# Output stage of a two-layer gated attention kernel: early low parts on VectorE, down bias on GpSimd

## The reference, cut to what matters

```python
def _bit_quant(w):
    scale = jnp.maximum(jnp.mean(jnp.abs(w)), EPS)
    return jnp.clip(jnp.round(w / scale), -1.0, 1.0)      # in the forward pass

# end of _L1_xattn_ref
x = x + jnp.tanh(g_xattn[1]) * (attn @ Wo.T + bo)
# _L1_ffn_ref(_layernorm(x))
h = jnp.einsum('bsd,fd->bsf', ln, _bit_quant(w1)) + b1     # 2048 hidden
h = jax.nn.gelu(h, approximate=False)
x = x + jnp.tanh(g_ffn[1]) * (jnp.einsum('bsf,df->bsd', h, _bit_quant(w2)) + b2)
```

## Time and profile before

| | us |
|---|---|
| three runs | 2008.91, 2006.67, 2000.90 |
| their median | 2006.67 |
| the profiled execution, its own time | 1998.72 |
| its span in the trace | 1996.9 |
| TensorE matmuls busy (share of the span) | 1913.5 (96%) |
| VectorE busy | 998.1 (50%) |
| ScalarE busy | 752.5 (38%) |
| GpSimd busy | 1098.9 (55%) |

### The profile page before, as it was taken

The page is one execution under the profiler, slowest core; times in us unless marked ns, Lnnn a source line. Parts: engine busy times, 40 slices in busy tenths (PEclk is TensorE's granted clock), DMA queues, the critical chain, the costliest instruction groups (busy, mean ns, idle before and its releaser), DMA issues. The chain is left out here.

```text
span 1996.9 us, 29500 instructions
## 1 busy us (share of the span) xinstructions
PE 1913.5 (96%) x10300; PEld 1606.3 (80%) x10300; DVE 998.1 (50%) x1670; ACT 752.5 (38%) x1147; POOL 1098.9 (55%) x986
## 2 busy tenths in 40 slices
PE   8999999999999999989999899998999997999998
PEld 6888888988888888967777799998777775778886
DVE  5446444745466444663333333333888876771111
ACT  4327343644336332632121221222444454434333
POOL 6765688549756777454116855640544435833333
PEclk9999999999999999999999999999999997999999
DMA  5231332223322423334136755532898666240000
GB/s 175 85 116 54 117 116 95 75 86 127 105 80 69 148 85 126 115 134 163 40 117 202 245 170 186 155 109 73 250 258 227 180 170 219 87 127 21 21 21 21
DMA packets 172283, 248.10 MB, mean 124 GB/s; under 512 B 44992, under 2 KB 69568, under 8 KB 172160
## 3 DMA queue, kind: packets, MB, share of 16 engines
q1 hardware_dynamic: 157072, 202.09, 32.1%
q0 software_dynamic: 9472, 34.09, 5.1%
q10 hardware_dynamic: 5616, 10.23, 1.3%
HBM read 179.77 MB, written 66.58 MB: 123 GB/s over the span
## 5 line engine op out<-in xcount | busy, mean ns | idle before, releaser
L262 POOL TENSOR_TENSOR a_w_hl<-a_w_raw,a_w_hl 128x512 fp32r<-128x512 f32 x232 | 303.9, 1342 | 140.9 <-ACT a_w_hl L341 140.9
L477 PE MATMUL a_proj<-a_c_hl,a_w_hl 128*128 128x512 f32 x768 | 180.5, 394 | 9.1 <-DVE a_w_hl L597 8.7
L477 PE MATMUL a_proj<-a_w_hl,a_c_hl 128*128 128x512 f32 x768 | 181.2, 392 | 0.0
L551 PE MATMUL a_proj<-a_w_hl,a_a_hl 128*128 128x512 f32 x768 | 178.7, 391 | 0.8 <-DVE a_a_hl L681 0.8
L477 PEld LDWEIGHTS a_proj<-a_c_hl,a_w_hl 128*128 128x128 f32 x768 | 144.1, 189 | 41.5 <-DVE a_w_hl L597 10.9
L477 PE MATMUL a_proj<-a_a_hl,a_w_hl 128*128 128x512 f32 x768 | 176.4, 390 | 0.0
L371 ACT ACTIVATE a_sq<-a_proj,a_vecs 128x512 f32<-128x512 f32 x128 | 88.1, 688 | 212.9 <-PE a_proj L477 143.5
L2642 POOL TENSOR_TENSOR f_a_hl<-f_act_sb,f_a_hl 128x512 fp32r<-128x512 f32 x64 | 86.1, 1347 | 148.9 <-ACT f_a_hl L2690 148.8
L477 PEld LDWEIGHTS a_proj<-a_a_hl,a_w_hl 128*128 128x128 f32 x768 | 143.6, 188 | 29.7
L341 ACT ACTIVATE a_w_hl<-a_w_raw 128x2048 fp32r<-128x2048 f32 x59 | 112.8, 1911 | 144.8 <-PE a_proj L477 106.7
L551 PEld LDWEIGHTS a_proj<-a_w_hl,a_a_hl 128*128 128x128 f32 x768 | 142.9, 188 | 30.2 <-issue 1.2
(11 more groups left out here) (269 smaller groups left out, 3494.5 us busy)
## 6 DMA issues: line engine op xcount, KB each, us to landing
a_w_raw<-in_a_vi_w SPq DMA_DIRECT2D x16, 1024.0 KB, 4.9
a_w_raw<-in_a_q_w SPq DMA_DIRECT2D x16, 1024.0 KB, 4.9
a_w_raw<-in_a_o_w SPq DMA_DIRECT2D x16, 1024.0 KB, 5.3
a_w_raw<-in_a_ki_w SPq DMA_DIRECT2D x15, 1024.0 KB, 5.7
spare<-in_b_gate_up POOLq DMA_DIRECT2D x32, 352.0 KB, 3.3
l_sorted_rows<-b_zeros SPq DMA_DIRECT2D x39, 256.0 KB, 3.7
spare<-l_sorted_rows SPq DMA_DIRECT2D x39, 256.0 KB, 3.2
l_expert_out<-spare ACTq DMA_DIRECT2D x39, 256.0 KB, 3.5
```

The costliest lines, as they stand in the source:

```text
L262: ins = pool.tensor_tensor(w_hl[:, s, 1, k], w_raw[:, s, k], f32(w_hl[:, s, 0, k]), ALU.subtract)
L477: mm = pe.matmul(proj[:, j, :], left, right, start=(k == 0 and n == 0), stop=(k == KC - 1 and n == 2))
L551: mm = pe.matmul(proj[:, j, :], a_hl[:, ap, k, j * P:(j + 1) * P], w_hl[:, i % 2, wp, k], start=(n == 0 and m == 0), stop=(n == 4 * G - 1 ...
```

## The change

Three things are altered in `l1_output_ffn`.

1. The low parts of chunks 4 to 7 are computed by VectorE (`early_low_part`) behind the statistics of tile 1, with a semaphore of their own (`a_early`), and no longer by GpSimd. The counts that SyncE and TensorE wait for are adapted.
2. The scaled down bias is added to the rows by GpSimd inside the feed-forward loop, tile m - 1 of the block ahead of the low part m, for m = 1 to 4. VectorE's addition behind the multiply-add goes away; its multiply-add now waits for GpSimd's addition (`y_biased`), and the store for the multiply-add (`y_added`).
3. Ahead of the loop GpSimd waits for the last normalised tile (`ln_done` 16) and for the scaled down bias (`const_done` 2).

```diff
--- before.py
+++ after.py
@@ -2518,6 +2518,8 @@
         a_in = [sem(f"a_in{s}") for s in range(RING)]
         a_high = sem("a_high")
         a_split = sem("a_split")
+        a_early = sem("a_early")
+        y_biased = sem("y_biased")
         o_ready = sem("o_ready")
         o_added = sem("o_added")
         ln_stats = sem("ln_stats")
@@ -2535,7 +2537,6 @@
         g_split = sem("g_split")
         y_ready = sem("y_ready")
         y_added = sem("y_added")
-        y_done = sem("y_done")
         x_out = sem("x_out")
 
         x2_t = x2.rearrange("(b n p) d -> b p n d", p=P, n=TPB)
@@ -2564,7 +2565,10 @@
             def load_chunk(n):
 
                 if n >= KC + RING:
-                    sp.wait_ge(a_split, n - RING + 1)
+                    if n - RING < AHEAD:
+                        sp.wait_ge(a_early, n - RING - KC + 1)
+                    else:
+                        sp.wait_ge(a_split, n - RING - (AHEAD - KC) + 1)
                 sp.dma_start(a_raw[:, n % RING, :], a_t[n % KC][n // KC]).then_inc(a_in[n % RING], 16)
 
             def load_piece(m):
@@ -2593,7 +2597,7 @@
                 load_piece(m)
             with sp.Fori(0, NBLK) as t:
                 for j in range(TPB):
-                    sp.wait_ge(y_done, TPB * t + j + 1)
+                    sp.wait_ge(y_added, TPB * t + TPB + j + 1)
                     sp.dma_start(out_t[j][t], y[:, bass.ds(TPB * t + j, 1), :]).then_inc(x_out, 16)
             sp.wait_ge(x_out, 16 * NT)
 
@@ -2623,8 +2627,6 @@
             pool.wait_ge(const_done, 1)
             add_bias(0)
             add_bias(1)
-            for n in range(KC, AHEAD):
-                a_low(n)
             for n in range(NT + 2):
                 if n < NT:
                     pool.wait_ge(ln_eps, 2 * n + 2)
@@ -2636,8 +2638,13 @@
                     add_bias(n + 2)
                 for m in chunk_beside(n):
                     a_low(m)
+            pool.wait_ge(ln_done, NT)
+            pool.wait_ge(const_done, 2)
             with pool.Fori(0, NBLK) as t:
                 for m in range(NG * FC):
+                    if 0 < m <= TPB:
+                        tile = y[:, bass.ds(TPB * t + m - 1, 1), :].rearrange("p a d -> p (a d)")
+                        pool.tensor_tensor(tile, tile, tg_b2[:], ALU.add).then_inc(y_biased, 1)
                     pool.wait_ge(g_high, NG * FC * t + m + 1)
                     pool.tensor_tensor(a_hl[:, 1, m % FC, :], act_sb[:, m % 2, :], f32(a_hl[:, 0, m % FC, :]),
                                        ALU.subtract).then_inc(g_split, 1)
@@ -2696,8 +2703,12 @@
             pe.matmul(m_ps[:], ones[:], sum2[:], start=True, stop=True).then_inc(mean_ready, 1)
 
             def project_out(n):
-                if n:
-                    pe.wait_ge(a_split, KC * (n // TPB + 1))
+                if n >= 2 * TPB:
+                    pe.wait_ge(a_split, KC * (n // TPB + 1) - (AHEAD - KC))
+                elif n >= TPB:
+                    pe.wait_ge(a_early, AHEAD - KC)
+                elif n:
+                    pe.wait_ge(a_split, KC)
                 if n >= 2:
                     pe.wait_ge(o_added, n - 1)
                 own = slice(n * P, (n + 1) * P)
@@ -2812,9 +2823,18 @@
                 dve.tensor_tensor(h_hl[:, 1, :, own], y_ps[:, 2 + n % 2, :].rearrange("p (k n) -> p k n", k=KC),
                                   f32(h_hl[:, 0, :, own]), ALU.subtract).then_inc(h_split, 1)
 
+            def early_low_part(n):
+                own = slice(n // KC * BLK, (n // KC + 1) * BLK)
+                dve.wait_ge(a_high, n + 1)
+                dve.tensor_tensor(h_hl[:, 1, n % KC, own], chunk_raw(n), f32(h_hl[:, 0, n % KC, own]),
+                                  ALU.subtract).then_inc(a_early, 1)
+
             for n in range(NT + 2):
                 if n < NT:
                     add_output(n)
+                if n == 1:
+                    for m in range(KC, AHEAD):
+                        early_low_part(m)
                 if n >= 2:
                     h_low_part(n - 2)
                 if n == ROUNDED[0]:
@@ -2832,11 +2852,10 @@
             with dve.Fori(0, NBLK) as t:
                 for j in range(TPB):
                     tile = y[:, bass.ds(TPB * t + j, 1), :].rearrange("p a d -> p (a d)")
+                    dve.wait_ge(y_biased, TPB * t + j + 1)
                     dve.wait_ge(y_ready, TPB * t + j + 1)
                     dve.scalar_tensor_tensor(tile, y_ps[:, j, :], tgs[:, 1:2], tile, ALU.mult, ALU.add)\
                         .then_inc(y_added, 1)
-                    dve.wait_ge(y_added, TPB * t + TPB + j + 1)
-                    dve.tensor_tensor(tile, tile, tg_b2[:], ALU.add).then_inc(y_done, 1)
 
 
 def build(nc, a, out):
```

## The result

The changed kernel took 2041.71 us in the median of four runs (2036.02 to 2045.48), the kernel before 2006.56 in four. The difference of the medians is 35.2 us. The ratio is 1.0179, with a 95% interval of 1.0162 to 1.0196: slower. The ratios given with an interval are taken over the runs and are not quotients of the two medians (here 1.0175); the two differ by up to 0.001.

The account below looks back on a forecast made before the run. TensorE, busy 96% of the span, was taken to bound the kernel's feed-forward loop. Terms 0.5 + 37.0 - 2.4 = +35.1 us on the 2006.67 median gave 2041.8 us, range 2031 to 2050.

Parts of the forecast that it names:

- Front: Before the feed-forward loop: chunk 8's load is issued 2.3 us later, mostly hidden by DMA backlog; +0.5 us, bounds 0 and +2.3.
- VectorE's four early subtractions: Before the loop: the four low parts moved to VectorE, 2.8 us, fit in 4.17 us of its idle time; no cost.
- End of the wait: At loop entry: VectorE's bias scaling, which GpSimd waits for, ends at 1793.5, paced by weight loads; bounds 1783.4 and 1799.6.
- rounding no faster than now: Rival, chance 0.10: loads, not GpSimd, set VectorE's total for the weight pieces; scaling ends at 1799.6, sum 6.1 us larger, 2047.9.
- Loads keep up: Rival, chance 0.04: weight loads never hold VectorE before the bias scaling, so the sum is 10.1 us less, 2031.7.
- GpSimd's pace after the wait: In block 1: low parts and additions start 1.25 us apart, the last lasts 1.29; fourth low part ready at 1802.4.
- Loop entry as a whole: TensorE stands idle before the first `down`; the first `down` group ends at 1804.3 against 1767.29: +37.0 us, bounds +26.9 and +43.1.
- Cold restart: After TensorE's 35 us idle, half clock for 3.4 us, covered by GpSimd's pace: 0; uncovered, 1.6 us more.
- Blocks 2 to 4: Later loop blocks: GpSimd's three additions before its fourth low part fit with 0.8 us slack before `down(3)`: 0.
- Additions overrun: Rival, chance 0.04: GpSimd additions take 1.65 us each, exceeding slack by 0.4 in each of three blocks: +1.2 us, 2043.0.
- Tail: After the last matmul: VectorE loses four additions, leaving four multiply-adds 0.79 us apart; -2.4 us, bounds -3.1 and -0.7.
- The spread of its own values: Whole kernel: the forecast as worked out, chance 0.76, runs from 2037 to 2046 by bounds before the loop and multiply-add spacing.

Follow-up runs that it names:

- the wait alone: Kernel before plus only GpSimd's two waits ahead of the feed-forward loop (`ln_done`, `const_done` 2), no operation moved: 2041.92 us against 2003.33, ratio 1.0196.
- the bias scaled early: The change, with VectorE scaling the down bias ahead of the last 14 roundings instead of behind them: 2005.46 us against 2003.33, ratio 1.0003.
- the wait at the first addition: The change, with the `const_done` wait moved inside the loop, between low parts 0 and 1 of block 1: stage 349.9 us in one execution.
- the loads reordered: The change with additions behind low parts 12 to 15, chunk 4's low part first, last 1 MB row load behind chunks 8 to 11: 1999.01 us, ratio 0.9974.

## Why the prediction was right

The forecast was 2041.8, measured 2041.7; that they meet to 0.1 us is luck, since single runs of the change span 9 us. The mechanism is no luck: the wait alone gives the whole loss, and with its count reached early the hole is gone. The stage shows how good the terms were: +35.1 forecast, +34.9 measured.

- **Front,** +0.5: +0.8 in the profiled pair. The issue 2.3 us later was right to 0.1 (14.2 against 11.9 us into the stage), and that the DMA backlog hides most of it. The runs say that all of it is hidden within the scatter of 1.4 us, so the term should have been 0 with that scatter.
- **VectorE's four early subtractions,** 2.8 us in idle time: 2.5 (1703.73 to 1706.24).

```profile
1703.73 2.59 DVE L2829 TENSOR_TENSOR f_h_hl<-f_a_raw,f_h_hl 128x512 fp32r<-128x512 f32 x4
1706.24 0.74 DVE L2808 SCALAR_TENSOR_TENSOR carry<-f_totals,f_tgs,carry 128x512 f32<-128x512 f32 x1
```

- **End of the wait:** with the start of the first rounding taken as zero, the scaling's end was worked out as 1793.5 - 1752.5 = 41.0 and came 1802.15 - 1761.98 = 40.2 later. The pace of the loads was right (pairs 5.9 on average against 6.05). The rival "rounding no faster than now" is out: no piece was stretched (0.75 and 1.28 us in all 14). "Loads keep up" is out as well: 11 load waits, 10.5 us.
- **GpSimd's pace after the wait,** 1.25 an operation: right; the fourth low part was ready 9.0 us after the scaling's end, worked out as 8.9.
- **Loop entry as a whole,** +37.0: 37.6 to the second `hidden` group, of which 0.8 is the front: 36.9.
- **Cold restart,** 0 in the change: right, since the group's end was set by GpSimd. That the low clock would last 3.4 us held only there (3 us); uncovered, in the run with the wait alone, it lasted nearly 5 and cost 2.6, not 1.6.
- **Blocks 2 to 4,** 0: right, the groups are 7.49 and 7.28 throughout. "Additions overrun" did not come: all 16 additions of the change took 1.27 to 1.29 us, none the 1.65 of that rival. The rival was about blocks 2 to 4; in block 1 the wait itself had moved the additions behind the rounding. With the wait gone and the scaling early they do overrun, in block 1 alone, by 3.2 us.
- **Tail,** -2.4: -2.8, by the last column of the table. The multiply-adds came 0.66 apart, not 0.79.
- **The spread of its own values,** "from 2037 to 2046": the bounds it gives for front and tail make 2040.6 to 2045.3. The stated range does not rest on it.

The Trainium skill ("SBUF — State Buffer", "Who interferes with whom") says that the pair of SBUF ports that VectorE and GpSimd share is an exclusive lock, and that a VectorE instruction with two SBUF inputs contends with a GpSimd instruction that reads SBUF. The rows of the run with the bias scaled early agree in kind: a GpSimd addition of 1.29 us takes 1.7 to 2.3 beside the rounding; no run here separates the ports from another cause. The prediction took its GpSimd pace of 1.25 us for the additions from rows without the rounding beside them. Behind the wait that held; it says nothing of the arrangement without the wait, where the same additions cost 3 us in block 1.

## What to carry to other kernels

A semaphore wait on an engine that serves others in order is paid by everything queued behind it: before adding one, read from the trace when its count is reached, not only how long the operation that gives it takes. Where an operation is moved to an engine as filler, put it where the other engine's work does not stretch it and where what is queued behind it is least urgent; here the same four additions cost 37 us with the wait ahead of them, 3 beside the rounding and 0 behind it. And compare a change inside one stage from that stage's own start, when what runs before it scatters by 10 us.

## What was not expected of the hardware

- The time at half clock after a restart was not one number: 3 us in the change, nearly 5 in the run with the wait alone, both after more than 30 us of idling; in the run with the wait at the first addition the clock was 0.50 still in the microsecond from 1808, 4.4 us after the restart at 1804.64, and 1.00 from 1810.
- The first `hidden` group took 7.75 to 10.2 us in different executions with the same instructions. The granted clock goes with it: it was 1.00 in the microsecond from 1754 in the run with the wait alone (7.75 us), and with the loads reordered 0.50 in that from 1759 and 1.00 only from 1761, more than five us into the group (10.1 us).
- A 256 KB load issued behind 2 MB of others at 11.9 us into the stage landed after 5.7, 6.7 and 7.1 us in three executions with identical code up to there. What makes this scatter was not looked into.
